# Stationary operands of the down products and of the output projection 64 bytes further in SBUF

## The reference

```python
x = x + tanh(g_xattn) * xattn(layernorm(x), ctx)   # 16 heads of 64, keys and values from ctx
x = x + tanh(g_ffn) * ffn(layernorm(x))

# the end of xattn: out is [b, s, 1024]
out = out @ Wo + bo                                # 1024 -> 256

# ffn: 8 experts, top 2, 1024 slots for each expert
h  = relu(einsum('ecd,ehd->ech', de, fc1_w) + fc1_b)   # 256 -> 1024
eo = einsum('ech,ehd->ecd', h, fc2_w) + fc2_b          # 1024 -> 256
```

## Time and profile before

| what | value |
|---|---|
| median of 3 runs | 1044.92 us (1044.9 to 1047.18) |
| profiled execution, its time | 1046.19 us |
| profiled execution, its span | 1044.5 us |
| mean granted TensorE clock | 0.991 of full |
| PE, PEld busy | 1000.2 us (96%), 863.3 us (83%) |
| DVE, ACT, POOL busy | 686.0 us (66%), 478.8 us (46%), 482.6 us (46%) |
| attention, then experts | about 645 us, then about 400 us |

### The profile page before, as it was taken

One profiled execution on the slowest core, in us unless ns is written; L12 is line 12 of the kernel. 1 busy time (PEld: TensorE's weight loads), 2 busy tenths in 40 slices (PEclk: granted clock), 3 DMA queues, 4 the chain that ended last, 5 costly groups with the idle time before them and its releaser, 6 DMA issues. The chain is left out here.

```text
span 1044.5 us, 21103 instructions
## 1 busy us (share of the span) xinstructions
PE 1000.2 (96%) x7314; PEld 863.3 (83%) x7314; DVE 686.0 (66%) x1607; ACT 478.8 (46%) x1502; POOL 482.6 (46%) x498
## 2 busy tenths in 40 slices
PE   6899999999999999999999997999999999999995
PEld 5678778778778878878878786799999999999995
DVE  6885895885885885886885855444555554444552
ACT  3663553553553653553563630434353543435351
POOL 7521071080170270260360244385757658585856
PEclk9999999999999999999999998999999999999998
DMA  8201110120021021021001001334426152433525
GB/s 247 82 20 43 42 61 1 40 61 20 20 60 37 4 60 40 0 60 60 0 1 61 2 5 48 121 58 109 105 73 155 28 140 43 123 58 100 129 48 65
DMA packets 49948, 63.42 MB, mean 61 GB/s; under 512 B 5976, under 2 KB 41714, under 8 KB 49906
## 3 DMA queue, kind: packets, MB, share of 16 engines
q1 hardware_dynamic: 37234, 45.41, 13.6%
q0 software_dynamic: 12672, 17.47, 9.8%
HBM read 46.45 MB, written 16.78 MB: 61 GB/s over the span
## 5 line engine op out<-in xcount | busy, mean ns | idle before, releaser
L727 ACT ACTIVATE work<-score,negmax 128x128 f32<-128x128 f32 x256 | 90.4, 380 | 78.9 <-DVE negmax L924 78.9
L1257 ACT ACTIVATE hid<-up,b 128x512 f32<-128x512 f32 x128 | 88.4, 690 | 80.8 <-PE up L1208 79.1
L1136 POOL DMA_INDIRECT out_dram<-eo,index_e x64 | 107.0, 1672 | 19.5 <-issue 19.5
L727 ACT ACTIVATE probs_odd<-score,negmax 128x128 f32<-128x128 f32 x256 | 90.4, 381 | 52.6 <-DVE negmax L924 52.6
L1309 DVE TENSOR_TENSOR eo_raw<-down,b 128x256 f32<-128x256 f32 x64 | 26.2, 425 | 133.1 <-PE down L1222 124.8
L348 POOL TENSOR_SCALAR var<-mv 128x4 f32<-128x4 f32 (+1 forms) x17 | 3.9, 228 | 221.5 <-DVE mv L779 215.3
L1302 DVE TENSOR_TENSOR hid_l<-hid,hid_h 128x512 fp32r<-128x512 f32 x128 | 88.7, 693 | 4.4
L1265 ACT ACTIVATE eo<-eo_raw,gate_e 128x256 f32<-128x256 f32 x64 | 31.0, 508 | 130.8 <-DVE eo_raw L1309 120.6
L680 ACT ACTIVATE q_sb<-proj 128x512 f32<-128x512 f32 x64 | 38.7, 605 | 108.9 <-PE proj L598 108.8
L1300 DVE CAST hid_h<-hid 128x512 fp32r<-128x512 f32 x128 | 54.9, 429 | 42.6 <-ACT hid L1257 37.8
L924 DVE TENSOR_REDUCE negmax<-score 128x4 f32<-128x512 f32 x128 | 81.9, 682 | 0.8 <-PE score L519 0.8
(11 more groups left out here) (217 smaller groups left out, 3078.1 us busy)
## 6 DMA issues: line engine op xcount, KB each, us to landing
w_raw<-fc1T_dram SPq DMA_DIRECT2D x9, 1024.0 KB, 5.4
w_raw<-fc_dram SPq DMA_DIRECT2D x9, 1024.0 KB, 9.2
rows<-x_dram SPq DMA_DIRECT2D x16, 512.0 KB, 4.3
out_dram<-rows SPq DMA_DIRECT2D x8, 512.0 KB, 2.8
xn_rows<-rows SPq DMA_DIRECT2D x8, 512.0 KB, 2.8
c_raw<-ctxT_dram SPq DMA_DIRECT2D x8, 256.0 KB, 3.7
c_raw<-ctxT_dram SPq DMA_DIRECT2D x16, 128.0 KB, 4.2
b<-fc2b_dram SPq DMA_DIRECT2D x9, 128.0 KB, 7.2
```

What stands on the lines that cost most here:

```text
L727: last = nc.scalar.activation(probs[j % 2][:, c, :], score[hh][:, b * P:(b + 1) * P], ACT.Exp, bias=negmax[:, j % 2, c:c + 1], accum_out=s ...
L1136: pool.indirect_dma_start(out=out_rows[:, :], out_offset=bass.IndirectOffsetOnAxis(ap=index_e[par][:, half * GB + i:half * GB + i + 1], ax ...
L1257: nc.scalar.activation(hid[m % 2][:, :], up[m % 2][:, :], ACT.Relu, bias=b1[par][:, m:m + 1]).then_inc(s_hid, 1)
```

## The change

Two tiles of 64 bytes that nothing reads or writes are allocated, one in front of `aT_h` in attention, one in front of `hid_h` in experts. All tiles behind them in their stage move by 64 bytes. No instruction is added, removed or moved: on each of the five engines the instructions stand in the same order as before.

```diff
 ROUND_UP = (20480 - 18656) // 4
+LINE_UP = 64 // 4
...
     pT = sb("pT", [P, 2, 2, TOK])
+    sb("line_up", [P, LINE_UP])
     aT_h, aT_l = sb("aT_h", [P, NP, TOK], f32r), sb("aT_l", [P, NP, TOK], f32r)
...
     hid = [sb(f"hid{n}", [P, TOK]) for n in range(2)]
+    sb("line_up_hid", [P, LINE_UP])
     hid_h, hid_l = sb("hid_h", [P, HK, TOK], f32r), sb("hid_l", [P, HK, TOK], f32r)
```

## The result

The changed kernel took 1035.53 us (median of 4 runs, 1034.84 to 1036.3), the kernel before, beside it, 1045.76 us (4 runs, 1044.9 to 1047.18). The ratio is 0.9901 with a 95% interval of 0.9884 to 0.9918: 10.2 us or 1.0% faster. Of the timed runs in this text one, the fourth of the later repeat of the changed kernel, took 3387.4 us for no reason that the record shows, and its ratio is taken from the other three.

A forecast was written before the change was run, and what follows sets the result against it. The prediction took PE's matmul pace to bound the kernel. All its terms were 0 and summed to 0, so the median was to stay at 1045.0 us, with a range of 1040 to 1054 us for 8 in 10.

The forecast's parts named there:

- The bound: Whole kernel: PE is busy 1000.2 of 1044.5 us with almost no waits, so time is the sum of its paces.
- The two streams: Down products (16 phases) and output projections (8), 96 matmuls each at 120 ns: 276.5 us, 26% of the time.
- All the terms beside the matmuls: Row tile 3's weight loads, DVE writes of the moved tiles, and instructions, order, waits and DMA issues: each taken as 0.
- rival 2: Down and output streams: row tile 3's loads cross a 2 KB multiple and slow it, 7.7 us, 1052.7 us; chance 0.07.
- rival 3: Down and output streams become uneven like the Q products, some 10 ns a step, 23 us, 1068 us; chance 0.06.
- Matmuls, 2304 of them: 0 ns each: Down and output streams: pace unchanged, from equal row tile paces; bounds 20.7 us gained to 30.6 us lost.
- no effect: Whole kernel: the change leaves the time at 1042 to 1048 us; chance 0.71.
- rival 1: Down and output streams: extra time comes from the stationary operand's start; steps fall to about 111 ns, 20.7 us; chance 0.13.
- The other witness: Warm-up matmuls on `ident`, 32 bytes off a multiple of 64: 0.112 us against 0.111, so an odd start costs nothing.
- the whole slack: Down and output matmuls: 9 ns between their 120 ns pace and the 111 ns a weight load needs.
- the addition of 13.3 ns: Float32r streams at full clock: each matmul pays 13.3 ns beside its columns, whatever their number.
- The weaker form: Down and output streams: only one row tile in four gains, 5.2 us; chance 0.03.

The follow-up runs named there:

- the run with the halves apart: Against the kernel before, only hid_h and aT_l put at a distance of 64, hid_l at 256, aT_h as before; 1041.67 us beside 1042.67.

## Why the prediction was wrong

**What held.** The bound: PE's pace is the time, and 11.1 of the 11.4 us came out of it. The two streams and their 2304 matmuls. All the terms beside the matmuls: DVE at 430, 692 and 681 ns, the waits, the order. Row tile 3, whose loads now go over a 2 KB multiple, runs like the others, so its 0 ns were right (rival 2 falls). No stream became uneven (rival 3 falls). The reading of the earlier trace rows that the multiple of 2 KB is not the reason: shown by the run with both operands moved and the one with the stationary operands back on the multiples. The gain isn't owed to leaving the multiples of 2 KB.

**The step that failed** is the first term, "Matmuls, 2304 of them: 0 ns each". Measured, it is a gain of 11.1 us, 4.8 ns each. It rested on the equal paces of the row tiles at 0, 512, 1024 and 1536 bytes. The prediction said itself that these can't rule out a reason that repeats every 512 bytes or less, then took them for three offsets tried out of four. They were one offset tried four times: the pattern repeats every 256 bytes, and every distance in the kernel before was 0. The equal paces weighed nothing against such a pattern, and the 0.71 that stood on them should have been close to an open question between "no effect" and rival 1. The other witness, the warm-up matmuls of the earlier trace rows, had stationary and moving operand in the same tile; by the run with both moved, that is the one change that can't show anything. And the prediction had a hint in its rows: loads of 192 ns in these streams and 188 in the up streams, "a difference that the pace doesn't show". In the changed kernel the loads fell to 188 where the pace fell to 113.3.

**Rival 1 was nearest to the mechanism**, at a chance of 0.13. That the gain comes from how the starts of the two operands lie to each other is shown; that their reads collide is still argued, since no run shows the reads. Its "for" held: an addition that is there only at full clock, and a phase that before can't show. Its "against" failed: it argued that two reads of different speed would meet at most offsets whatever the start. The runs show the reverse, a pace that depends on where the two begin, with values between 113.3 and 120.0 ns at eight places. Each step starts a load and a matmul together; that this fixes how the two reads lie to each other would be a reason, and isn't shown.

**Its size was wrong too.** It took the whole slack down to the pace of a load, 9 ns x 2304 = 20.7 us. The least that any placement gave is 113.3 ns, 6.7 ns below 120, and half of the addition of 13.3 ns stays: 16 of 32 cycles. About 15 of the 24 streams got that and 9 got 2.2 ns: (15 x 6.7 + 9 x 2.2) / 24 = 5.0 ns, x 2304 = 11.5 us, near the 11.1 measured. The weaker form, a gain in one row tile of four (5.2 us), came nearer to the 10.2 us than the full one, but by the wrong way: the gain comes by phase, and all four row tiles of a phase have it.

**On the rules that were weighed.** The Trainium skill, "SBUF — State Buffer", section "Who interferes with whom", says that PE has a read port for the moving operand and one for loading weights, independent of each other. These runs differ: the pace of the same instructions goes from 113.3 to 120.0 ns with nothing but the distance of the two operands' starts. The gap by the formula of the Trainium skill, "TensorE: Matmul & The Clock Gate", section "Back-to-back issue gap", 109.2 ns for 256 columns, is one that no placement here reached. The section gives that formula for an isolated matmul, without its weight load, which the prediction didn't say; so the 10.8 ns between the two were no measure of what a placement could win. And the count of 16-byte lines, which the prediction took from the Trainium skill, "SBUF — State Buffer", section "Specifications (TRN2)", and held against rival 1, is the same at all eight distances while the pace differs: the count alone isn't the addition.

**What stays open.** Which reads meet, since neither the own nor the next operand explains the run with the halves apart. What sets a stream to 113.3 or 117.8 ns. The traces narrow it to the first step: of the 128 down phases at distances of 64, 320 and 576 all 60 at 117.8 ns begin with a step of 200 or 201 ns, and 65 of the 68 at 113.3 with one of 205 to 207; the other three begin with 201 or 202 and come to 113.3 within five steps. What makes the first step long or short isn't known, nor why the runs with a changed up phase ahead of them had 113.3 ns in nearly all down phases (two of them, at a distance of 64) or 117.8 in all (at 576). Why up products lose at each distance that was tried but 256. Why DVE's last addition starts late beside POOL's indirect DMA in some executions, and whether that goes with the chip.

## What to carry to other kernels

Where PE's pace is the bound, and a float32r stream of 256 columns loads a new stationary operand for each matmul, look at the distance of the two operands' starts in a partition, modulo 256 bytes: large tiles laid one behind another have a distance of 0, with 160 the slowest place here, and a pad of 64 bytes before the stationary tile gave 1% of the kernel. Check it by the steps in one phase, not by the total, and leave the streams of 512 columns at a distance of 0. Equal paces at several offsets say nothing of a pattern that repeats with the step between them: ask first which places the kernel has never been in.

## What the runs showed of the hardware

- A float32r stream of 256 columns at full clock takes 120.0 ns a matmul when both operands start at the same place modulo 256 bytes, whatever the place (0 and 64 tried), and 113.3 to 120.0 ns by the distance, as in the map above.
- Once past its first few steps a stream holds one pace for its 96 matmuls, even where its operands differ in distance (117.8 ns with one or two of three moved). At a distance of 64 there are two such paces, 113.3 and 117.8 ns, in the same kernel and from execution to execution; at 192 one stream of 48 had 113.3 and not 117.8, at 96 the last of eight 118.6 and not 117.3.
- Past the first steps, loads of the next operand last 192 ns in all steps of a stream at a distance of 0, 187 or 188 ns in all steps of a stream at 64 with 113.3 ns, and 192 at one line of three in a stream at 64 with 117.8 ns.
- Products of 512 columns (up) take 226.7 ns at a distance of 0 and 256, and with their moving operand on by 64 bytes 228.9 (one phase 233.3), by 128 bytes 232.2, by 448 bytes 233.3 ns: every tried shift but the one of 256 makes them slower.
- A load that goes over a 2 KB multiple costs nothing that can be seen: the loads of row tile 3 do so in the changed kernel, and its steps are those of the other row tiles in the same phase.
- DVE's addition out of PSUM started up to 1.9 us late beside an indirect DMA of POOL (1.57 us) in five of 16 traces and at once in the others, with the same instructions in the same order.
